# Reordering the front of a two-layer cross-attention kernel: loads in two queues, K by halves, the output operand on GpSimd

## What is computed

```python
# layer 0: 16 heads of 16 features; only batch 0's attention is used
q, k, v = heads(x @ Wq.T), heads(ctx @ Wk.T), heads(ctx @ Wv.T)
att = softmax(q @ k.T / sqrt(16)) @ v
y = x + att[0]                          # added to every batch
# layer 1, for each batch
X  = layernorm(ctx, w1, b1)
F  = layernorm(y, w2, b2)
A  = softmax(F @ X.T / 16) @ X          # only A @ fc1_w.T is needed
h  = gelu(A @ fc1_w.T + fc1_b)          # 4 hidden values per token
C  = h @ fc2_w.T + fc2_b                # rank 4, plus a bias
N3 = layernorm(C, w3, b3)
S  = softmax(N3 @ N3.T / 16) @ N3
out = F + gamma2 * (C + gamma1 * S)
```

## Time and profile before

| | |
|---|---|
| median of 3 runs | 248.01 us (246.8 to 248.02) |
| the profiled execution: time, span | 246.86 us, 245.1 us |
| TensorE matmuls | 214.2 us, 87% of the span |
| VectorE | 198.0 us, 81% |
| ScalarE | 148.9 us, 61% |
| GpSimd | 124.4 us, 51% |
| granted TensorE clock, mean | 0.957 |
| chain that ended last | TensorE 55%, VectorE 28% |

### The profile page before, as it was taken

One profiled execution on the slowest core, in us unless ns is written; L12 is line 12 of the kernel. 1 busy time (PEld: TensorE's weight loads), 2 busy tenths in 40 slices (PEclk: granted clock), 3 DMA queues, 4 the chain that ended last, 5 costly groups with the idle time before them and its releaser, 6 DMA issues.

```text
span 245.1 us, 4980 instructions
## 1 busy us (share of the span) xinstructions
PE 214.2 (87%) x1758; PEld 154.2 (63%) x1758; DVE 198.0 (81%) x391; ACT 148.9 (61%) x284; POOL 124.4 (51%) x184
## 2 busy tenths in 40 slices
PE   6989989677999999999999899999978569999750
PEld 6766548446878779697787787867645225554320
DVE  6888858899999978789899999733558958998764
ACT  2167856226778678596787968846775326666310
POOL 6000096776999999969698939200002522222220
PEclk9999999999999999999999999999999759999955
DMA  6990000242455514455243000000000022444566
GB/s 186 366 350 3 1 4 0 93 143 109 173 171 148 161 56 155 174 168 174 82 151 113 3 1 3 0 1 3 0 3 1 0 88 86 173 175 174 190 238 257
DMA packets 14712, 26.81 MB, mean 109 GB/s; under 512 B 1760, under 2 KB 1760, under 8 KB 14688
## 3 DMA queue, kind: packets, MB, share of 16 engines
q1 hardware_dynamic: 14688, 26.50, 31.2%
HBM read 18.11 MB, written 8.39 MB: 108 GB/s over the span
## 4 chain that ended last, share of the span: by engine, by line
PE 55%; DVE 28%; issue 8%; ACT 4%; POOL 2%; DVEq 0%; POOLq 0%; ACTq 0%
PE psum L981 15%; PE psum L918 7%; DVE bn L381 6%; DVE xN L401 6%; PE psum L989 5%; PE psum L873 5%; DVE nm L564 3%; PE psum L1019 3%; PE psum L1095 3%; PE psum L931 2%; DVE nmax L524 2%; PE psum L1001 2%; PE psum L946 2%; PE psum L959 2%; PE psum L888 2%
## 5 line engine op out<-in xcount | busy, mean ns | idle before, releaser
L981 PE MATMUL psum<-XT,Fall 128*128 128x256 f32 x256 | 60.9, 381 | 1.8 <-ACT Fall L763 1.8
L981 PEld LDWEIGHTS psum<-XT,Fall 128*128 128x128 f32 x256 | 46.1, 190 | 7.2 <-ACT Fall L763 2.2
L656 POOL TENSOR_SCALAR cN<-cN,nmean,rstd 128x256 f32<-128x256 f32 x64 | 38.5, 614 | 2.4 <-POOL rstd L643 2.3
L636 POOL TENSOR_TENSOR xN<-xN,tgt 128x512 f32<-128x512 f32 x28 | 35.7, 1278 | 1.6 <-DVE xN L401 1.6
L401 DVE TENSOR_SCALAR xN<-xN,bn,rstd 128x256 f32<-128x256 f32 x64 | 33.8, 571 | 0.7 <-POOL rstd L643 0.7
L786 ACT ACTIVATE PT<-psum 128x512 f32<-128x512 f32 x32 | 19.2, 599 | 24.3 <-PE psum L989 24.2
L700 POOL CAST sC<-co 128x160 bf16<-128x160 f32 x8 | 2.6, 322 | 61.6 <-DVE co L581 61.6
L793 ACT ACTIVATE E<-psum,nmax 128x256 f32<-128x256 f32 x64 | 26.8, 475 | 10.9 <-DVE nmax L524 10.9
L524 DVE TENSOR_REDUCE nmax<-psum 128x2 f32<-128x512 f32 x32 | 22.0, 686 | 13.7 <-PE psum L981 13.2
L643 POOL TENSOR_TENSOR rstd<-vps,minus_half 128x8 f32<-128x8 f32 (+1 forms) x16 | 25.0, 1564 | 15.4 <-DVE vps L392 15.3
L760 ACT ACTIVATE XT<-psum,b1s,w1s 128x512 f32<-128x512 f32 x32 | 23.1, 794 | 3.8 <-PE psum L918 3.8
(11 more groups left out here) (157 smaller groups left out, 348.5 us busy)
## 6 DMA issues: line engine op xcount, KB each, us to landing
cN<-ctx SPq DMA_DIRECT2D x32, 256.0 KB, 2.9
xN<-x SPq DMA_DIRECT2D x32, 256.0 KB, 4.2
out<-Fall SPq DMA_DIRECT2D x32, 256.0 KB, 2.3
x0T<-x0t SPq DMA_DIRECT2D x1, 256.0 KB, 2.6
wqT<-wqt SPq DMA_DIRECT2D x1, 256.0 KB, 2.9
c0T<-c0t SPq DMA_DIRECT2D x1, 256.0 KB, 3.7
wkT<-wkt SPq DMA_DIRECT2D x1, 256.0 KB, 4.8
wvT<-wvt SPq DMA_DIRECT2D x1, 256.0 KB, 5.0
```

The costliest lines, as they stand in the source:

```text
L636: pool.tensor_tensor(xN[:, b % SLOTS, :], xN[:, b % SLOTS, :], tgt2[:, :, :].rearrange("p t d -> p (t d)"), ALU.add).then_inc(y_ok, 1)
L656: pool.tensor_scalar(own, own, nmean[:, p % 4, NT * m + t:NT * m + t + 1], root_of(p, 0, m, t), ALU.add, ALU.mult)\
L981: last = pe.matmul(bank[SBANK1[b % 3]][:, t * N:(t + 1) * N], Fall[:, b, c, t * P:(t + 1) * P], XT[:, p % 4, c, m * N:(m + 1) * N], start= ...
```

## The change

- **Loads.** `wqT`, `par`, `wkT` and `wvT` stay in SyncE's queue in this order; `x0T` and `c0T` go to ScalarE's queue. The first eight context batches are loaded ahead of the first eight of x.
- **GpSimd.** `meanw` is its first constant, and the fillers run on it instead of `ident` (five first, two after the mean). The output operand is made here in 17 small steps, behind the constants; VectorE's three parts are gone.
- **K by halves.** Each half has its own bank and raises `k_mm`; VectorE masks the first half (`masked(0)`) before the first head pair, and the second one (`masked(1)`) behind that pair's maxima. V's projections go to banks 0 and 1 and stand behind the scores of head pairs 0 and 2; ScalarE copies them at head pairs 1 and 3.
- **Roots by pair.** The variances of context pairs 0, 1 and 2 are made at head pairs 1, 3 and 5, and GpSimd takes each root and normalizes each pair by itself.
- **Start of the second stage.** `project(0)`, `operand_products` and `project_back(0)` stand between the key and query transposes of pair 0 and replace most of 11 fillers. VectorE copies `Q` and `K` there. `add(5)` on GpSimd waits until VectorE has normalized batches 2 and 3. The statistics of x's batch 5 and the variances of pair 2 move behind `maximum(0)`.
- **VectorE's order in the second stage.** `maximum(b)`, `values` and `saved` come ahead of the statistics of batch b + 6; before, they came behind them.

```diff
@@ sync
+        sp.dma_start(wqT[:, :, :], wqt).then_inc(q_in, 16)
         sp.dma_start(par[:, :], params).then_inc(par_in, 16)
-        for dst, src, arrived in ((x0T, x0t, q_in), (wqT, wqt, q_in), (c0T, c0t, k_in), (wkT, wkt, k_in),
-                                  (wvT, wvt, v_in)):
-            sp.dma_start(dst[:, :, :], src).then_inc(arrived, 16)
+        sp.dma_start(wkT[:, :, :], wkt).then_inc(k_in, 16)
+        sp.dma_start(wvT[:, :, :], wvt).then_inc(v_in, 16)
+        for src, dst, arrived in ((c_d, cN, c_in), (x_d, xN, x_in)):
+            for b in range(SLOTS):
+                sp.dma_start(dst[:, b, :], src[b, :, :]).then_inc(arrived[b], 16)
@@ vector
+        def masked(o):
+            dve.wait_ge(k_mm, o + 1)
+            for e, m in enumerate(("even", "odd")):
+                dve.tensor_scalar(kTm[:, e, o, :], bank[(1, 5)[o]][:, 0:N], c_(m), None, ALU.mult).then_inc(kT_ok, 1)
+
+        masked(0)
...
+        def first_variances(p):
+            dve.wait_ge(st_ok, 2 * p + 2)
+            dve.tensor_scalar(nmean[:, p, :].rearrange("p (m t) -> p m t", t=NT),
+                              bn[:, p, 0, :, :].rearrange("p m (t k) -> p m t k", t=NT)[:, :, :, 1],
+                              -1.0, None, ALU.mult).then_inc(vps_first, 1)
+            dve.tensor_scalar(vps[:, p, 0, :].rearrange("p (m t) -> p m t", t=NT),
+                              bn[:, p, 0, :, :].rearrange("p m (t k) -> p m t k", t=NT)[:, :, :, 2],
+                              1.0 / D, EPS, ALU.mult, ALU.add).then_inc(vps_first, 1)
...
             if p < NHP:
+                if p == 0:
+                    masked(1)
                 if p < 2 * EARLY:
                     statistics(p, 0)
...
+                if p in (1, 3, 5):
+                    first_variances(p // 2)
...
         add(2)
         add(3)
+        dve.wait_ge(qk_mm, 1)
+        link(dve.tensor_copy(Q[:, :], bank[7][:, 0:(H + 1) ** 2]))
+        link(dve.tensor_copy(K[:, :], bank[7][:, 64:64 + U * U]), "QK")
         normal(0)
...
         normal(3)
-        statistics(5, 1)
-        variances(2)
...
         for b in range(B):
             k, m, q = b // 2, b % 2, b // 4
+            maximum(b)
+            if b % 4 == 2:
+                values(q)
+            if b % 4 == 3 and q >= 1:
+                saved(q - 1)
+            if b == 0:
+                statistics(2 * EARLY - 1, 1)
+                variances(EARLY - 1)
             if k + 3 < PAIRS:
                 statistics(b + 6, 0)
                 statistics(b + 6, 1)
                 if m == 1:
                     variances(k + 3)
-            maximum(b)
-            if b % 4 == 2:
-                values(q)
-            if b % 4 == 3 and q >= 1:
-                saved(q - 1)
             if k + 2 < PAIRS:
                 normal(b + 4)
-            if b == 18:
-                output_operand(2)
@@ gpsimd
+        pool.memset(meanw[:, :], 1.0 / D).then_inc(consts, 1)
         pool.memset(ident[:, :], 0.0).then_inc(consts, 1)
...
+        pool.wait_ge(zero_ok, 4)
+        pool.wait_ge(alg, ALG["prods"])
+        step(pool.tensor_tensor(g12[:, :], c_("g1"), c_("g2"), ALU.mult))
...
         def add(b):
             pool.wait_ge(x_in[b % SLOTS], 16 * (b // SLOTS + 1))
...
+            if b == 5:
+                pool.wait_ge(zy_ok, 8)
...
+        for p in range(EARLY):
+            pool.wait_ge(vps_first, 2 * p + 2)
+            pool.tensor_tensor(rstd[:, p, 0, :], vps[:, p, 0, :], minus_half[:, 0:2 * NT], ALU.pow).then_inc(root_first, 1)
+            normal(2 * p)
+            normal(2 * p + 1)
@@ scalar
+        act.dma_start(x0T[:, :, :], x0t).then_inc(q_in, 16)
+        act.dma_start(c0T[:, :, :], c0t).then_inc(k_in, 16)
...
         for p in range(NHP + 1):
+            if p in (1, 3):
+                values_copied(p // 2)
...
         for p in range(EARLY):
             evacuate(p, 0)
+        turned_values(0)
         evacuate(0, 1)
@@ tensor
-                pe.matmul(bank[b][:, 0:P], ident[:, :], ident[:, :], start=True, stop=True)
-        pe.wait_ge(consts, 4)
-        keep_busy(7, 4)
+                pe.matmul(bank[b][:, 0:P], meanw[:, :], meanw[:, :], start=True, stop=True)
+        pe.wait_ge(consts, 1)
+        keep_busy(5, 4)
...
+        keep_busy(2, 4)
...
         for p in range(EARLY):
             turned(p, 0)
-        keep_busy(11, 7)
...
+        project(0)
+        operand_products()
+        keep_busy(3, 0)
+        project_back(0)
+        keep_busy(4, 0)
         turned(0, 1)
```

More of the change, by code:

```diff
@@ L629, in _, with step @@
         pool.memset(sC[:, :, SC:SLOT], 0.0).then_inc(zero_ok, 1)
+        oc = [0]
+        def step(ins):
+            ins.then_inc(operand_ok, 1)
+            oc[0] += 1
+            pool.wait_ge(operand_ok, oc[0])
+        a5 = c_("a5").rearrange("p (c k) -> p c k", c=DC)
+        pool.wait_ge(zero_ok, 4)
+        pool.wait_ge(alg, ALG["prods"])
+        step(pool.tensor_tensor(g12[:, :], c_("g1"), c_("g2"), ALU.mult))
+        for c in range(DC):
+            step(pool.tensor_scalar(Rt[:, c, 0:H], a5[:, c, 0:H], c_("g2", c), None, ALU.mult))
+            step(pool.tensor_scalar(Rt[:, c, H:CO], MT[:, c, :], g12[:, c:c + 1], None, ALU.mult))
+            step(pool.tensor_scalar(Rcut[:, c, 0:1], a5[:, c, H:H + 1], c_("g2", c), None, ALU.mult))
+            step(pool.tensor_tensor(Rt[:, c, CO - 1:CO], Rt[:, c, CO - 1:CO], Rcut[:, c, 0:1], ALU.add))
+        for part in range(2):
+            to = stR[:, :, part, :]
+            step(pool.tensor_copy(slots(to, CO, SLOTS_L[0]), repeated(Rt[:, :, :], 3)))
+            step(pool.tensor_tensor(Rcut[:, :, :], Rt[:, :, :], to[:, :, 0:CO], ALU.subtract))
+            step(pool.tensor_copy(slots(to, CO, SLOTS_L[1]), repeated(Rcut[:, :, :], 2)))
+            step(pool.tensor_tensor(to[:, :, 5 * CO:6 * CO], Rcut[:, :, :], to[:, :, 3 * CO:4 * CO], ALU.subtract))
+        ALG["stR"] = oc[0]
         def add(b):
@@ L811, in _ @@
             exponentials(b)
-            if b % 4 == 1:
+            if b % 4 == 1 and q >= 1:
                 turned_values(q)
@@ L882, in _ @@
         last.then_inc(mean_mm, 1)
-        for arrived, n, w, src, b, done in ((q_in, 32, wqT, x0T, 0, q_mm), (k_in, 32, wkT, c0T, 1, k_mm)):
-            pe.wait_ge(arrived, n)
-            for o in range(2):
-                for c in range(DC):
-                    last = pe.matmul(bank[b][:, o * N:(o + 1) * N], w[:, c, o * P:(o + 1) * P], src[:, c, :],
-                                     start=c == 0, stop=c == DC - 1)
-            last.then_inc(done, 1)
+        keep_busy(2, 4)
+        pe.wait_ge(q_in, 32)
+        for o in range(2):
+            for c in range(DC):
+                last = pe.matmul(bank[0][:, o * N:(o + 1) * N], wqT[:, c, o * P:(o + 1) * P], x0T[:, c, :],
+                                 start=c == 0, stop=c == DC - 1)
+        last.then_inc(q_mm, 1)
+        pe.wait_ge(k_in, 32)
+        for o in range(2):
+            for c in range(DC):
+                last = pe.matmul(bank[(1, 5)[o]][:, 0:N], wkT[:, c, o * P:(o + 1) * P], c0T[:, c, :],
+                                 start=c == 0, stop=c == DC - 1)
+            last.then_inc(k_mm, 1)
         def operand_products():
@@ L915, in turned @@
                 for m in range(2):
-                    pe.wait_ge((zc_ok, zy_ok)[side], 2 * (2 * p + m) + 2)
+                    if side == 0:
+                        pe.wait_ge(zc_ok, 2 * (2 * p + m) + 2)
+                    else:
+                        pe.wait_ge(zy_ok, 2 * (2 * p + m) + 2)
                     for t in range(NT):
@@ L934, in _ @@
             if p == 0:
+                pe.wait_ge(v_in, 16)
+                value_projection(0)
+            if p == 2:
                 value_projection(1)
@@ L1139, in _ @@
                 score(b)
-            if b % 4 == 1 and q < QUADS:
+            if b % 4 == 1 and 1 <= q < QUADS:
                 project(q)
             if b % 4 == 2:
-                project_back(q)
+                if q >= 1:
+                    project_back(q)
                 if q >= 1:
```

67 lines of the change are left out of this document (14 added, 53 removed).

## The result

The median went from 248.01 us (5 executions, 246.53 to 248.18) to 249.42 us (5 executions, 249.37 and more), 1.4 us or 0.6% slower; the ratio of the two kernels is 1.008 with a 95% interval of 1.004 to 1.012. The forecast was 246.7 us, with a range of 244.2 to 249.4. One execution of after took 256.85 us at a mean granted clock of 0.915 (the others 0.945 to 0.959), and executions like it are left out of all ratios here and kept in all medians. The profiled execution took 249.37 us, span 247.5 us, against 246.86 and 245.1 us of before: 2.4 us of span to explain.

The account below looks back on a forecast made before the run. TensorE was taken to set the pace in the second stage, with VectorE and GpSimd close behind. The terms -2.0 + 0.3 + 0.1 + 0.8 - 0.5 = -1.3 us gave 246.7 us, range 244.2 to 249.4.

Parts of the forecast that it names:

- Front, -2.0: Up to layer 0's first scores: earlier fillers and loads and half of K start the scores at 9.15, 2.0 us earlier.
- rival 2: Front: the clock stays low through the projections; sum +0.1 to +1.5 us, 248.1 to 249.5 us; chance 0.12.
- Loop, +0.3: Loop over head pairs in the front: the first pair's variances stand in a place without slack, costing 0.3 us.
- Start of the second stage, +0.1: Start of second stage: gain of removed contention is spent waiting for `add(5)` and in GpSimd's queue; 0.1 us lost.
- rival 1: Start of the second stage keeps its gain, -1.5 us there and no steady loss; 244.3 us; chance 0.20.
- Steady part, +0.8: Middle of second stage: every second pair's keys late by about 0.15 us, five times; 0.8 us lost.
- Late part, -0.5: Second stage from b = 20: maxima first are no longer made late by the algebra; 0.5 us gained.
- rival 3: Steady part: VectorE's new order becomes the bound, +3.5 instead of +0.8; 249.4 us, beyond that 251; chance 0.20.
- Third stage: The stage after the second one, to the end: untouched by the change, predicted difference 0.

Follow-up runs that it names:

- b4: The kernel before with only VectorE's second-stage order changed (maximum, values, saved ahead of the statistics): median 249.69 us, ratio to before 1.009.
- a3: The changed kernel with nine fillers instead of five ahead of the mean: median 247.35 us, ratio to before 1.000.
- b1: The changed kernel with nine first fillers and VectorE's old order, `par` still behind `wqT`: median 246.86 us, ratio to before 0.998.
- a2: The changed kernel with VectorE's old order in the second stage (statistics and variances ahead of the maximum): median 248.35 us, ratio to before 1.004.
- c3: The kernel before with `meanw` as first constant and five early fillers on it instead of seven on `ident`: median 248.32 us, ratio to before 1.005.
- a1: The changed kernel with `par` issued ahead of `wqT` in SyncE's queue: median 248.79 us, ratio to before 1.004.
- b3: b1 with `add(8)` on GpSimd waiting until VectorE has normalized batch 4: median 247.35 us, ratio to before 0.999.
- c4: b2 with `add(8)` on GpSimd waiting until VectorE has normalized batch 4: median 246.61 us, ratio to before 0.998.
- c1: b2 with the maximum ahead of the statistics for batches below 20 only: median 247.68 us, ratio to before 1.003.
- b2: The changed kernel with nine first fillers, `par` ahead of `wqT` and VectorE's old order: median 246.33 us, ratio to before 0.997.
- c2: b2 with the maximum ahead of the statistics for even batches only: median 249.54 us, ratio to before 1.007.

## Why the prediction was wrong, step by step

**Front, -2.0: the step that failed first.** `meanw` first, half a mask (0.88), the output operand on GpSimd (17 steps, 8.11 to 13.69 us) came as predicted. Two terms didn't. The loads: `par` landed at 4.8, not 4.1, and `x0T` and `wqT` at 4.4 and 4.6, not 3.9; I had carried over durations of one queue to two queues that run side by side. Q's projection waited for `par` and what stands behind it, and started at 6.71 instead of 5.5: 1.2 us. And the clock: I kept the rise where it was and gave rival 2 (248.1 to 249.5) a chance of 0.12. Q and half of K took 3.9 us instead of 2.8: 1.1 us. With 0.2 at the masks these are the 2.5 us between -2.0 and +0.51. How much of the clock's 1.1 us belongs to the change and how much to the execution stays open, for b4's unchanged front lost as much. Over many executions the early filler counts: a3 adds four to after and gains 0.8%, b1 adds four to a2 and gains 0.6%, and c3, with two fewer in before and an earlier start, loses 0.5%. Where the clock state is alike, the reordering itself does give what I counted: the rise at 7.94 goes with first scores at 12.23 in b4, and at 7.83 with 10.44 in a1 (-1.8 us).

**Loop, +0.3, and the way to score(0):** measured +0.1.

**Start of the second stage, +0.1.** With before's order it is -0.06 (a2): `normal(2)` and `normal(3)` took 1.38 us, and the 2.2 us went into the wait for `add(5)`, GpSimd's queue and the held `normal(4)`, as followed. The order put `root(3)` 0.6 us later, as I had counted (10.55 us behind score(0), 9.95 in a2), but I let other gains take up all but 0.1 us of it, and the stretch lost 0.45. Each of `normal(4)`'s two instructions began behind an add and ended 0.15 us behind it (the second at 56.12, the add at 55.97). The Trainium skill ("SBUF — State Buffer", section "SBUF: two separate sides") says that whichever of VectorE and GpSimd starts first has the shared ports for its whole instruction, and that the other is blocked. The trace agrees: 2.62 us beside two adds, and 1.09 in b3 and c4, where one add overlaps. Of rival 1's gain at this place (1.5 us) no run has more than c4's 0.95.

**Steady part, +0.8.** Measured +0.04. The count itself held: in after `root(6)` starts 4.31 us behind `score(7)` (80.72 - 76.41), I had 4.29, before had 2.35. GpSimd ends the pair's second batch 5.40 us later:

```profile
80.72 1.74 POOL L663 TENSOR_TENSOR rstd<-vps,minus_half 128x8 f32<-128x8 f32 x1 [1.60 <-DVE vps L379]
...
84.99 1.13 POOL L676 TENSOR_SCALAR cN<-cN,nmean,rstd 128x256 f32<-128x256 f32 x2
...
86.00 1.05 PE L952 MATMUL psum<-ident,cN 128*128 128x128 f32 x8
```

That is 86.12, and TensorE starts at 86.00, but with two transposes of the pair's first batch. The 0.12 us fell inside these. All the slack of 1.8 us was eaten, and nothing was lost yet.

**Late part, -0.5: the wrong sign.** I said that maxima first would make the maxima earlier. At the place that I had priced, `maximum(26)` starts 4.77 us behind its scores, 3.56 in before, and from score(26) to score(27) it took 4.92 us, neither the 4.38 that I forecast nor before's 4.85. Where VectorE has no slack, maxima can't come earlier: `maximum(25)` starts 4.48 us behind `score(25)` in after (148.16 - 143.68) and 4.22 in a2 (147.44 - 143.22), because whatever now stands behind maximum(24) stands ahead of maximum(25). What the order does move is the variances: against a2, pair 13's root comes 2.1 us later behind the scores and pair 15's 2.4. Beyond the slack of 1.8 us that leaves 0.3 and 0.6, about what was lost at batches 24 and 28 (0.3 and 0.7). I had seen this in the steady part and stopped at b = 7, where VectorE has no algebra. That is rival 3's mechanism at another place than its own, with +1.16 where rival 3 had added 2.7 in the steady part. b4 shows it without the rest of the change, with TensorE waiting for GpSimd's keys twice, 1.1 us in all. c1, which takes the order back from batch 20 on, is free of it from score(24) on.

**Third stage:** +0.17, as said.

**In sum** rivals 2 and 3 came together. Each was named and priced alone, and the range's upper end of 249.4 allowed for one of them. The failed steps are the -2.0 us of the front and the sign of the -0.5 us of the late part. Why one execution's clock rises at 4 and another's at 10 us behind nearly the same fillers (a3, b1 and b2) stays open; the few-column products of the mean stand among the fillers in all versions, and a front without them was not tried.

## What to carry to other kernels

Before you move a step behind a wait, write down for each engine how far ahead of its consumer it runs, at the busiest place and not at a typical one: here 1.8 us of slack was spent everywhere, and was missed only where more work stood in the same list. In this kernel work that runs ahead (statistics) was better off ahead of work that waits for the bounding engine (the maximum), and changing the order between iterations cost more still. Filler at the start is part of the schedule: if a load behind which it ends moves by 1 us, let the filler follow. And where the clock differs between executions, compare many of them: a3's trace points the wrong way, and c4's shows a gain that its median doesn't have.

## What the runs showed of the hardware

- The start of the high clock differed between executions of the same front: 5.32 and 7.94 us in before and b4; 10.55, 5.87 and 9.80 in a3, b1 and b3; 4.12, 4.39, 6.32 and 3.83 in b2, c1, c2 and c4, which have `par` first besides. The first scores moved with it, from 9.2 to 12.6 us over all runs.
- A 20 KB load took 3.6 us from issue to landing behind one of 256 KB in its queue with a second queue busy, 2.5 us as first in its queue beside the second one (a1), and 1.8 us in before.
- In the third stage the stretch at 1.2 GHz was 10.2 us long in nine of the profiled executions, b2's among them, 13.7 in b1's, 20.5 in b4's and c1's, and 30.7 in a3's and c2's; windows of the two kernels from 200 to 210 us (columns as in the earlier trace rows), b2 first:

```profile
200.00:210.00 10.00, 9.75 (x101) 4.88 (x95) 7.94 (x11) 6.06 (x11) 1.50 (x5) 0.90 0.28 105
```

```profile
200.00:210.00 10.00, 10.00 (x66) 4.77 (x66) 5.48 (x8) 4.36 (x8) 1.49 (x5) 0.50 0.16 58
```

The clock column is 0.90 and 0.50, and TensorE gets through 101 and 66 matmuls. From score(31) to the end c1 took 3.3 us more than b2, and no edit here was meant to touch that.
